# One VectorE bias for two score banks in the first six tiles of a gated cross-attention kernel

## What is computed

```python
x = x + tanh(g_xattn) * xattn(layernorm(x), ctx)
x = x + tanh(g_ffn) * ffn(layernorm(x))

# xattn, 16 heads of 32 columns
q = rms_norm(linear(x, q_w, q_b)) * norm_q_w
k = rms_norm(linear(ctx, k_w, k_b)) * norm_k_w
v = linear(ctx, v_w, v_b)
probs = softmax(q @ k.T / sqrt(32))      # for each head
out = linear(probs @ v, o_w, o_b)

# ffn, weights made ternary in groups of 64
h = relu(x @ ternary(W_fc).T) ** 2
out = rms_norm(h) @ ternary(W_proj).T
```

## Time and profile before

| | |
|---|---|
| median of three executions | 920.4 us |
| the profiled execution | 920.16 us, of which 918.3 us are its span |
| TensorE busy | 878.6 us, 96% |
| ScalarE busy | 798.8 us, 87% |
| VectorE busy | 710.3 us, 77% |
| GpSimd busy | 560.5 us, 61% |

### The profile page before, as it was taken

The page is one execution under the profiler, slowest core; times in us unless marked ns, Lnnn a source line. Parts: engine busy times, 40 slices in busy tenths (PEclk is TensorE's granted clock), DMA queues, the critical chain, the costliest instruction groups (busy, mean ns, idle before and its releaser), DMA issues.

```text
span 918.3 us, 22391 instructions
## 1 busy us (share of the span) xinstructions
PE 878.6 (96%) x7536; PEld 532.6 (58%) x7633; DVE 710.3 (77%) x1546; ACT 798.8 (87%) x1608; POOL 560.5 (61%) x616
## 2 busy tenths in 40 slices
PE   8687899999999999999999999999999999999998
PEld 5333465555665666656556666555566665556675
DVE  7999999878788787878788787878788787867301
ACT  6998999899899888889989888899898888989573
POOL 3222255776676766667666766667677666656476
PEclk9797899999999999999999999999999999999999
DMA  9958665676676676667666866566667656654501
GB/s 370 208 121 198 147 163 103 100 138 123 127 119 125 127 139 109 106 119 128 127 116 130 132 117 102 119 128 127 120 131 130 116 104 120 124 107 79 82 12 47
DMA packets 319890, 115.78 MB, mean 126 GB/s; under 512 B 305184, under 2 KB 305440, under 8 KB 318240
## 3 DMA queue, kind: packets, MB, share of 16 engines
q1 hardware_dynamic: 319776, 114.34, 63.6%
HBM read 30.67 MB, written 8.39 MB: 43 GB/s over the span
## 4 chain that ended last, share of the span: by engine, by line
PE 76%; ACT 4%; issue 2%; DMA 1%; POOL 1%; DVE 1%; SPq 0%; POOLq 0%; ACTq 0%; DVEq 0%
PE mix_pair L594 11%; PE up_pair L578 10%; PE up_pair L579 10%; PE mix_pair L593 8%; PE score_pair L532 5%; PE score_pair L531 5%; PE score_pair L533 5%; PE mix_pair L531 3%; PE mix_pair L532 3%; PE mix_pair L533 3%; PE score_ps L532 2%; PE score_ps L531 2%; PE score_ps L533 2%; PE score_pair L662 2%; ACT big L1030 1%
## 5 line engine op out<-in xcount | busy, mean ns | idle before, releaser
L578 PE MATMUL up_pair<-ft_all,w 128*128 128x256 f16 x960 | 215.9, 274 | 1.5 <-ACT h_all L1024 0.6
L579 PE MATMUL up_pair<-ft_all,w 128*128 128x256 f16 x960 | 216.0, 274 | 0.0
L2185 POOL TENSOR_TENSOR big<-h_all,big 128x512 f16<-128x512 f32 x128 | 154.2, 1205 | 57.0 <-ACT h_all L1033 38.9
L594 PE MATMUL mix_pair<-w,big 128*128 128x512 bf16 x464 | 175.9, 379 | 7.0 <-issue 4.1
L2195 POOL TENSOR_TENSOR h_all<-h_all,hh_sb 128x512 f32<-128x512 f32 x112 | 143.3, 1279 | 28.1 <-ACT hh_sb L1051 26.7
L593 PE MATMUL mix_pair<-w,big 128*128 128x512 bf16 x383 | 145.2, 379 | 0.2 <-POOL big L2185 0.2
L2140 POOL TENSOR_TENSOR ln_rstd<-ln_in,minus_half 128x1 f32<-128x1 f32 x64 | 46.0, 718 | 112.5 <-issue 90.8
L578 PEld LDWEIGHTS up_pair<-ft_all,w 128*128 128x128 bf16 x960 | 94.0, 98 | 18.4 <-DMA ft_all<-x_rows 1.2
L579 PEld LDWEIGHTS up_pair<-ft_all,w 128*128 128x128 bf16 x960 | 94.1, 98 | 15.8
L1093 ACT ACTIVATE score_ps<-score_ps,exp_bias,exp_scale 128x128 f32<-128x128 f32 x256 | 94.2, 440 | 0.0
L1093 ACT ACTIVATE score_pair<-score_pair,exp_bias,exp_scale 128x128 f32<-128x128 f32 x256 | 93.5, 429 | 0.3 <-DVE exp_bias L1644 0.2
(11 more groups left out here) (236 smaller groups left out, 2304.1 us busy)
## 6 DMA issues: line engine op xcount, KB each, us to landing
x_sb<-in_x SPq DMA_DIRECT2D x32, 256.0 KB, 3.2
ctx_sb<-in_ctx_t SPq DMA_DIRECT2D x32, 256.0 KB, 3.3
out<-out_sb SPq DMA_DIRECT2D x31, 256.0 KB, 3.5
big<-in_w_proj_t SPq DMA_DIRECT2D x4, 1024.0 KB, 5.6
big<-in_w_fc_t SPq DMA_DIRECT2D x2, 1024.0 KB, 7.6
pt<-p_rows SPq DMA_TRANSPOSE x128, 3.2
big<-in_wq_t SPq DMA_DIRECT2D x1, 1024.0 KB, 4.9
big<-in_wk_t SPq DMA_DIRECT2D x1, 1024.0 KB, 7.4
```

The source lines that it names most:

```text
L578: nc.tensor.matmul(dst[:, half], w, ft[i][:, c, :], start=(c == 0), stop=False)
L579: last = nc.tensor.matmul(dst[:, half], w, ft[i][:, C + c, :], start=False, stop=(c == C - 1))
L594: last = nc.tensor.matmul(dst[:, cols], ht_lo[i][:, row], w2[:, m, cols], start=False, stop=(m == M - 1))
L2185: nc.gpsimd.tensor_tensor(ht_lo[i][:, rows], h_sb[k % 3][:, :], ht_hi[i][:, rows], ALU.subtract).then_inc(hlo_ready, 1)
```

## The change

For tiles 0 to 5 VectorE calls a new function, `score_tops_by_two`, in place of `score_tops`. It takes the maxima of two banks one directly behind the other, then waits for both and makes the eight columns of `exp_bias` in one instruction, which raises `bias_ready` by 2. From tile 6 on `score_tops` stays.

```diff
+            def score_tops_by_two(t):
+                dve.wait_ge(s_done, t + 1)
+                if t == 0:
+                    dve.wait_ge(exp_scale_ready, 1)
+                for b in (0, 2):
+                    n, heads = 4 * t + b, slice(4 * b, 4 * b + 8)
+                    need(dve, bias_ready, n - 2)
+                    for i in range(2):
+                        nc.vector.tensor_reduce(m_top[:, 4 * (b + i):4 * (b + i) + 4],
+                                                score_ps[b + i][:, :].rearrange("p (u k) -> p u k", k=P), AX.X,
+                                                ALU.max).then_inc(top_ready, 1)
+                    dve.wait_ge(top_ready, n + 2)
+                    need(dve, exp_ready, n - 2)
+                    nc.vector.tensor_scalar(exp_bias[:, heads], m_top[:, heads], minus_scale[:, :], LOG_P_SCALE,
+                                            ALU.mult, ALU.add).then_inc(bias_ready, 2)
...
-            score_tops(0)
+            score_tops_by_two(0)
...
-            score_tops(5)
+            score_tops_by_two(5)
```

More of the change, by code:

```diff
@@ L1928, in _ @@
             ternary_signed(2)
-            score_tops(1)
+            score_tops_by_two(1)
             ternary_clip(3)
@@ L1961, in _ @@
             context_lo(3, 1)
-            score_tops(2)
+            score_tops_by_two(2)
             fc_top_of()
@@ L1998, in _ @@
             ternary_final(7)
-            score_tops(3)
+            score_tops_by_two(3)
             context_lo(4, 0)
@@ L2040, in _ @@
             ternary_half(27)
-            score_tops(4)
+            score_tops_by_two(4)
             probs_lo(4, 0)
```

## The result

The kernel with the change takes 923.94 us (median of 7 executions, 921.81 to 924.87); the kernel before, timed with it, 921.17 us (median of 7, 919.91 to 922.74). The ratio is 1.0028, 95% interval 1.0017 to 1.0038: 2.6 us slower, with an interval of 1.6 to 3.5. The interval excludes no change, though the difference is just under the 0.3% that I had called the least that a measurement can tell, and the time lies 0.3 us above my range. The sign held, and so did the mechanism in tiles 0 and 4; the sum of +1.1 was less than half of what was lost, because two steps were missing in tiles 1 and 5.

A forecast was written before the change was run, and what follows sets the result against it. VectorE and ScalarE were taken to bound tiles 0 to 4, TensorE tile 5 onward. Terms +0.35 + 0.21 + 0 + 0 + 0.55 + 0 = +1.1 us on the 920.4 median gave 921.5; range 918.6 to 923.6.

The forecast's parts named there:

- the sum of +1.1: Tile terms for tiles 0 to 5 added: +0.35 + 0.21 + 0 + 0 + 0.55 + 0 us.
- The price is paid by the first bias: In each changed tile, the first bias completes 0.60 us later, and ScalarE's first exponential waits for it.
- Rival (a): VectorE's saving of 0.52 us a tile survives at five tiles, 2.6 us in all: 917.8 us; chance 0.18.
- Rival (b): Effects cancel between tiles and tile 4's bias meets no GpSimd sum: -0.4 to +0.4 us, 920.4; chance 0.20.
- Rival (c): TensorE's clock rises too late for tile 1's projection: +2.4 us on top of 1.1, 923.9 us; chance 0.12.
- The sign that I had named for it: TensorE having a stretch at 1.2 GHz over a microsecond longer or shorter than before.
- VectorE's cost: Maxima and biases of a tile on VectorE: 1.46 us a pair, 2.92 a tile instead of 3.44, saving 0.52.
- Tile 0: ScalarE's exponentials and copies come later, so VectorE's difference is late: +0.35 us, bounds 0 and +0.6.
- Tile 1: ScalarE shows the bias's whole 0.60 delay; VectorE's differences wait for its copies: +0.21 us, bounds -0.2 and +0.6.
- Tiles 2 and 3: VectorE's gain becomes waiting, for ScalarE's copy or TensorE's output product: 0 for both, bounds -0.5 and +0.5 each.
- Tile 4: Bias waits for GpSimd's sum, delaying ScalarE, VectorE's difference and TensorE's matmul: +0.55 us, bounds -0.2 and +1.1.
- Tile 5: TensorE bounds; fewer biases take less from GpSimd, the later first one delays ScalarE: 0, bounds -0.3 and +0.3.

The follow-up runs named there:

- tile 1 alone: Against the kernel before, maxima and biases two banks at a time in tile 1 only; measured -0.2 us (-1.3 to +0.8).
- tile 0 alone: Against the kernel before (921.15 us), maxima and biases two banks at a time in tile 0 only; the text given states no time of its own.
- the late first bias: Against the kernel before, tiles 0 to 5 put banks 0 and 1's biases behind two maxima, keeping all four biases; 923.00 us against 920.95, ratio 1.0024.
- groups 1, 1, 2: Against the kernel before, tiles 0 to 5 take banks 0 and 1 singly, banks 2 and 3 as a pair; 920.82 us against 920.58, ratio 1.0007.
- tile 4 alone: Against the kernel before, maxima and biases two banks at a time in tile 4 only; 922.66 us in a single execution.

## Why the prediction was right in kind and too small in size

**The steps that failed** are the terms of tiles 1 and 5. For tile 1 (+0.21) I ended the path at VectorE's last difference; the runs show +0.75, over half of it behind that, where the last transposition now lands 3.8 to 3.9 us after its issue instead of 3.1. For tile 5 I put 0, taking the later first bias and the two missing ones for all that mattered; the runs show +0.48, because VectorE's mask now starts beside GpSimd's sum, which takes 1.24 instead of 0.73. The other terms were of the right kind and near in size.

**The mechanism.** "The price is paid by the first bias" held: the variants with a later first bias in four tiles or more lose, the one that keeps it early doesn't, and VectorE's saving is found again as waiting for ScalarE's copy. Rival (a) is out: even where VectorE saved most, nothing of it survived. Rival (b) is out by the interval. Rival (c) is out as far as it was put: `k_raw` starts 0.58 later behind T0 than before (14.72 us, 45.57 less 30.85, against the 14.14 from 30.28 to the 44.42 of the earlier trace rows), the 0.53 of the late difference and 0.05 more, and not 2.4. Where the clock rose earlier the difference is much the same: 14.18 and 14.19 with the change in tile 0, 13.53 to 13.64 with the old code. The sign that I had named for it did appear: by the granted clock of one-microsecond windows TensorE ran at 1.2 GHz from about 32.9 to 43.1 in the profile after and from 35.1 to 41.9 before, 3.4 us longer, and 10.2 us again in the second profile after. But it does not go with the change in tile 0: with tile 1 alone the stretch is as long, with tile 0 alone 6.8. So that sign was badly chosen. What sets these stretches is not shown.

**VectorE's cost** was 0.12 off a tile. I took 0.73 from a maximum to its bias out of the earlier trace rows; behind the second of two maxima it is 0.78 (1.38 less the 0.60 between maxima), and 0.14 follow. A pair costs 1.52, not 1.46. A bias that waits for its maximum costs 0.18 over the pitch of 0.60 behind a pair, where it was 0.13 behind a single one. The Trainium skill says in "VectorE: DVE Perf Modes", section "The DRAIN you can't avoid", that a semaphore behind each operation costs nothing extra. Its example is a row of eight copies, with a semaphore behind each or behind the last alone, and it gives no price for an instruction that waits for the one before it. Here the bias waits for its maximum, and the trace shows 0.73 to 0.79 for that against 0.60.

**Tile 0**: +0.35 forecast, +0.53 measured at the difference (5.14 against 4.61). The bias started 0.06 later than I worked out, and ScalarE began 0.10 behind its end in place of the 0.03 that I allowed. A miss in size, at the right step.

**Tile 1**: +0.21 forecast, +0.75 measured (T1-T2 23.5 to 23.7 against 22.6 to 22.8). This is the term that failed most, by a step that I left out. The last difference came +0.32 behind T1 (9.61 against 9.29), where I had worked out +0.21. I ended the tile there. But behind the difference stand SP's transposition and TensorE's product with it. That product starts 0.31 later too. It had no wait for the transpositions in the two executions before; in all four profiles with this tile's maxima in pairs it has one, 0.23 to 0.42 us, and ScalarE's `v_both` behind it comes 14.93 to 15.12 behind T1 instead of 14.22. The last transposition of the tile, before and then after:

```profile
L363 SPq DMA_TRANSPOSE pt<-p_rows x1: 1290/1290/1290, 66.4 to 66.4; - x1
DMA to landing us min/median/max: 3.1/3.1/3.1
```

```profile
L363 SPq DMA_TRANSPOSE pt<-p_rows x1: 1293/1293/1293, 67.8 to 67.8; - x1
DMA to landing us min/median/max: 3.9/3.9/3.9
```

So lateness alone does not make the wait: the issue is 0.3 later and so is the product, and before the change the transposition had landed some 0.3 us ahead of its first matmul (13.35 against 13.68 behind T1). What uses that up is the landing, 3.8 to 3.9 us behind the issue in those four profiles and 3.1 to 3.4 in the ten others. With the late first bias, where it is issued later still (10.65 behind T1 against 10.56), it lands after 3.2 us, the product has no wait, and T1-T2 is 23.12. Why the landing takes longer in just those four isn't shown. It isn't the clock: the second execution after and the kernel with groups 1, 1, 2 had nearly the same granted clock from 72 to 84 us and differ by 0.88 in T1-T2.

**Tiles 2 and 3**: 0 forecast for both; T2-T3 is between 0.0 and +0.5 over before, T3-T4 0.2 to 0.3 under it. Within the bounds, and near nothing together.

**Tile 4**: +0.55 forecast, +0.65 measured. The bias of 0.91 was forecast as "some 0.9", ScalarE's wait of 1.20 as 1.2. The rule that whoever issues first keeps the shared port to the end, cited in the forecast from "SBUF — State Buffer" of the Trainium skill, agrees in three more places: biases of 0.91, 0.89 (with tile 4 alone) and 1.30 us that end with the sum they ran into.

**Tile 5**: 0 forecast, +0.48 measured, and above my bound of +0.3. I asked what the bias takes from GpSimd and not what VectorE's earlier arrival would bring beside it. The same section of the Trainium skill says that a VectorE instruction with two inputs in SBUF contends with GpSimd instructions that read SBUF; I had read it for the bias alone. The trace agrees in 0.73 against 1.24 for the sum beside the mask. Had the sum waited for the whole mask, as by the rule above, it would have taken 0.64 + 0.73 = 1.37; it ended 0.60 behind the mask.

Together: 0.53 + 0.75 + 0.2 - 0.25 + 0.65 + 0.48 = 2.4, where the forecast had 1.1. Of the 1.3 between them, tiles 1 and 5 make 1.0.

**What stays open.** The end of the program gave back 1.2 us in the profiled execution: before, TensorE waits 0.78 and 0.43 us for transpositions at 858.42 and 859.32, and after it does not. From `h_ms` to the end of the span the fourteen profiles take 752.4 to 755.2 us, with both kernels on both sides, so I take this for the executions' own scatter. Why T0-T1 comes in two kinds I can only tie to the clock of that execution, and what decides it isn't shown; nor whether the change makes one kind more frequent, for the timed executions without a profile do not tell theirs.

## What to carry to other kernels

A saving on the busiest engine is worth nothing if it delays the first result that the next engine waits for; with the merged instruction last in the group the loss was gone here, though nothing was gained. Follow a delay through the transfer behind it, and look up how long before its use the data landed: 0.3 us of room was used up here by a transposition that took 0.8 longer. And where VectorE and GpSimd both work from SBUF, every instruction that comes earlier or later gets new neighbours: look at what starts beside each, in the tiles where "nothing changes" as well.

## What I had not expected of the hardware

- A four-column VectorE `tensor_scalar` took 0.23 us or 1.30 us by 0.08 us of difference in its start: ahead of GpSimd's sum at 160.17 against 160.25, or with it at 162.47. In a program as tight as this one, changes elsewhere decide such cases.
- The reverse exists too: a GpSimd sum of 128x256 went from 0.73 to 1.24 us when a VectorE product of two SBUF tiles started 0.04 ahead of it.
- Four, eight and sixteen columns of such a bias all took 0.23 us where no sum of GpSimd's ran beside them.
- The DMA transposition of the last bank of tile 1 landed 3.1 to 3.4 us after its issue in ten profiles and 3.8 to 3.9 in four.
- Two executions of one kernel had TensorE's clock rise and fall at different times in the first 55 us, and differed by 1.4 us there (25.82 and 27.24), while each of the four steps from T1 to T5 repeated within 0.17.
